# An attention stage's hand-placed pieces moved within the round, one output bank and three projection banks

## The reference, cut to what matters

```python
x = L0_attn_x                                   # 16 batches, 512 rows, 256 features
xn = _layernorm(x)
x = x + _L0_attn_ref(xn, ...)  + _L0_ffn_ref(xn, ...)
# _L0_ffn_ref:
x = x + mla(rmsnorm(x, w_ln1), ...)             # 16 heads of 16, causal softmax attention from low-rank
                                                # latents, with rotary halves, then W_o
x = x + moe(rmsnorm(x, w_ln2), ...)             # a shared expert on each row, and 2 of 7 routed experts
# _L0_attn_ref: a selective state-space scan (convolution, softplus, 512 steps of a clipped state)
```

## Time and profile before

| what | value |
| --- | --- |
| three executions | 4342.56, 4370.46, 4334.35 us |
| the profiled execution | 4341.7 us, its span 4339.9 us |
| mean granted clock of TensorE | 0.939 |
| PE, DVE, ACT, POOL busy, whole span | 86%, 68%, 58%, 51% |
| attention, 0 to 1710 us: PE busy | 1397.9 us |
| attention, 0 to 1710 us: DVE, ACT, POOL busy | 794.8, 650.9, 542.0 us |
| end of rounds 0 and 13 | 200.5 and 1499.1 us |

### The profile page before, as it was taken

One profiled execution on the slowest core, in us unless ns is written; L12 is line 12 of the kernel. 1 busy time (PEld: TensorE's weight loads), 2 busy tenths in 40 slices (PEclk: granted clock), 3 DMA queues, 4 the chain that ended last, 5 costly groups with the idle time before them and its releaser, 6 DMA issues. The chain is left out here.

```text
span 4339.9 us, 70850 instructions
## 1 busy us (share of the span) xinstructions
PE 3742.1 (86%) x22264; PEld 2767.9 (64%) x22264; DVE 2956.6 (68%) x5456; ACT 2513.7 (58%) x6505; POOL 2196.6 (51%) x1115
## 2 busy tenths in 40 slices
PE   5888888888888874899969999998999998999986
PEld 2344444444444442777758888887888887888876
DVE  3454454555444522222259999999999999999998
ACT  1443343434343441233358888888888888888874
POOL 3223333333333322000038788778778778878774
PEclk8899998999898987999989999999999999999998
DMA  3322222222232312666622212212222222222221
GB/s 91 98 80 84 80 92 86 88 80 81 79 101 81 93 46 75 199 208 208 211 92 98 88 68 100 93 66 97 93 70 93 93 81 82 93 88 75 93 83 38
DMA packets 286365, 417.03 MB, mean 96 GB/s; under 512 B 78261, under 2 KB 250678, under 8 KB 263672
## 3 DMA queue, kind: packets, MB, share of 16 engines
q1 hardware_dynamic: 273048, 381.12, 27.2%
q0 software_dynamic: 12288, 33.57, 2.2%
q10 hardware_dynamic: 864, 0.10, 0.0%
HBM read 330.63 MB, written 83.17 MB: 95 GB/s over the span
## 5 line engine op out<-in xcount | busy, mean ns | idle before, releaser
L1536 POOL TENSOR_TENSOR m_ub<-m_Bb,m_dtx 128x2048 f32<-128x2048 f32 x254 | 1156.9, 4566 | 280.3 <-PE m_Y L1904 176.4
L1645 ACT ACTIVATE m_dA<-m_dt,m_a_neg 128x128 f32<-128x128 f32 x4096 | 1211.1, 388 | 129.4 <-DVE m_S L1756 129.0
L1904 PE MATMUL m_Y<-m_ub,m_ident 128*128 128x128 f32 x8192 | 955.8, 278 | 62.4 <-DVE m_ub L1733 62.0
L1904 PEld LDWEIGHTS m_Y<-m_ub,m_ident 128*128 128x128 f32 x8192 | 939.3, 194 | 73.1 <-DVE m_ub L1733 72.8
L543 ACT ACTIVATE f_pt<-f_X 128x512 f32<-128x512 f32 (+1 forms) x704 | 371.8, 555 | 730.3 <-PE f_X L845 699.1
L618 DVE TENSOR_REDUCE f_nm<-f_Y 128x1 f32<-128x512 f32 (+3 forms) x896 | 434.0, 531 | 378.3 <-PE f_Y L845 354.1
L1748 DVE SCALAR_TENSOR_TENSOR m_PR<-m_dA,m_S 128x512 f32<-128x512 f32 x512 | 355.9, 695 | 25.7 <-POOL m_ub L1536 7.4
L1748 DVE SCALAR_TENSOR_TENSOR m_S<-m_dA,m_PR 128x512 f32<-128x512 f32 x512 | 354.8, 693 | 12.0
L1756 DVE CUSTOM_DVE_ANT_1 m_S<-m_S,m_ub 128x512 f32<-128x512 f32 x512 | 353.3, 690 | 0.6 <-issue 0.6
L1756 DVE CUSTOM_DVE_ANT_1 m_PR<-m_PR,m_ub 128x512 f32<-128x512 f32 x512 | 353.3, 690 | 0.2 <-DVE m_PR L1748 0.2
L828 PE MATMUL f_Y<-f_kst,f_qst 96*128 96x512 bf16 (+3 forms) x1024 | 256.2, 331 | 109.0 <-DVE f_nm L618 90.4
(11 more groups left out here) (234 smaller groups left out, 6369.2 us busy)
## 6 DMA issues: line engine op xcount, KB each, us to landing
m_Bb<-m_bc_dram SPq DMA_DIRECT2D x64, 1024.0 KB, 4.6
m_Cb<-m_bc_dram SPq DMA_DIRECT2D x64, 1024.0 KB, 6.4
f_parts_dram<-f_parts SPq DMA_DIRECT2D x32, 768.0 KB, 4.1
f_kst<-f_parts_dram SPq DMA_DIRECT2D x192, 128.0 KB, 2.6
f_qst<-f_parts_dram SPq DMA_DIRECT2D x192, 128.0 KB, 2.6
e_rows<-sorted_rows SPq DMA_DIRECT2D x70, 256.0 KB, 2.8
e_wg<-Wg SPq DMA_DIRECT2D x70, 256.0 KB, 2.9
e_wu<-Wu SPq DMA_DIRECT2D x70, 256.0 KB, 4.0
```

The lines of the kernel that those rows point to most:

```text
L1536: pool.tensor_tensor(ub[:, h, i, :, :], Bb[:, s, :, :], dtx[:, m, None, s * SN:(s + 1) * SN].to_broadcast([P, NST, SN]), ALU.mult).then_in ...
L1645: last = act.activation(dA[:, h, i, n, :], dtt[:, par, m, s * SN:(s + 1) * SN], ACT.Exp, scale=a_neg[:, m, n:n + 1])
L1904: last = pe.matmul(Y[:, i * SN:(i + 1) * SN], ident[:, :], ub[:, h, 1 + i, n, :], start=False, stop=(n == NST - 1), skip_group_check=True)
```

## The change

- **Pieces cut and moved.** T, ht and route become two pieces each, kq four for each head group, wo four. Nearly all places change: `d` goes from places 51 and 55 to 3 and 5 of the next round (stage -2), T from 15 to 8 and 9, lat from 18 to 12, kq of group 0 from 21 and 24 to 14, 16, 18, 18, kq of group 1 from 45 and 47 to 20, 22, 33, 33, wo from 25 to 25, 27, 29, 31, ht from 33 to 38 and 39, g and u from 37, 39, 42, 43 to 46, 49, 52, 55, rank from 40 to 52, nmt from 53 to 56, pfx from 47 to 58, keep from 32 and 58 to 27 and 44. scat (12 and 19), ym1 (18) and nm (50) stay.
- **Statistics a round earlier.** `xload` and `bn` work on batch n+3, at places 18 and 59; POOL's scalars of that norm are a kind of their own, `bnc`, at place 0 of the next round. There is one more round, -3, and rounds 2 to 11 are the loop; 12 and later are written out.
- **Banks.** One O bank instead of two, three Z banks instead of two. `oc` of a group now comes after the third s2 item of the next group instead of the sixth, and the first pv of a group waits for the copy of the group before. With it the pieces so, sl, rp, ro, rl, ym of the first pair of groups start at 35 instead of 39.
- **Numbering.** `place` counts each bank's uses by itself, and each round starts at bank 0 of each ring.

```diff
-    BANKS = {ring: [pb(f"f_{ring}{i}", [P, SEQ]) for i in range(2)] for ring in ("X", "Y", "Z")}
-    O = [pb(f"f_O{i}", [P, SEQ]) for i in range(2)]
+    DEPTH = {"X": 2, "Y": 2, "Z": 2, "Z": 3}
+    BANKS = {ring: [pb(f"f_{ring}{i}", [P, SEQ]) for i in range(DEPTH[ring])] for ring in ("X", "Y", "Z")}
+    O = pb("f_O", [P, SEQ])
...
-                if kb == 1 and g > 0:
-                    S2_ITEMS.append(("oc", g - 1, 0))
+            if n == 2 and kb == 0 and g > 0:
+                S2_ITEMS.append(("oc", g - 1, 0))
...
-    STAGE["scat"] = -2
+    STAGE.update({"scat": -2, "d": -2, "xload": 3, "bn": 3})
...
-    for n, kind, i, j in ((0, "xload", 0, 0), (0, "mvx", 0, 0), (0, "sl1", 1, 0), (1, "stack1", 1, 0), (4, "mvs", 0, 0), (6, "rp1", 1, 0), (7, "ro1", 1, 0), (8, "bn", 0, 0),
-                          (11, "h1", 0, 0), (12, "scat", 0, 0), (12, "rl1", 1, 0), (13, "h1a", 0, 0), (15, "T", 0, 0),
-                          (18, "lat", 0, 0), (18, "ym1", 1, 0), (19, "scat", 1, 0), (21, "kq", 0, 0), (24, "kq", 0, 1), (25, "wo", 0, 0),
-                          (26, "split", 0, 0), (28, "mid", 0, 0), (29, "h2", 0, 0), (30, "h2a", 0, 0), (31, "xrload", 0, 0),
-                          (32, "keep", 0, 0), (33, "ht", 0, 0), (35, "route", 0, 0), (36, "lg", 0, 0), (36, "xn", 0, 0), (37, "g", 0, 0), (37, "stack", 0, 0),
-                          (39, "u", 0, 0), (40, "rank", 0, 0), (42, "g", 1, 0), (43, "u", 1, 0), (45, "kq", 1, 0),
-                          (47, "kq", 1, 1), (47, "pfx", 0, 0), (49, "split", 1, 0), (50, "nm", 0, 0), (51, "d", 0, 0), (53, "mid", 1, 0), (53, "nmt", 0, 0),
-                          (55, "d", 1, 0), (58, "keep", 1, 0)):
+    for n, kind, i, j in ((0, "mvx", 0, 0), (0, "bnc", 0, 0), (0, "sl1", 1, 0), (1, "stack1", 1, 0), (3, "d", 0, 0), (3, "h1", 0, 0), (4, "mvs", 0, 0), (5, "d", 1, 0), (5, "h1a", 0, 0),
+                          (6, "rp1", 1, 0), (7, "ro1", 1, 0), (8, "T", 0, 0), (9, "T", 1, 0), (12, "scat", 0, 0), (12, "rl1", 1, 0), (12, "lat", 0, 0),
+                          (14, "kq", 0, 0), (16, "kq", 0, 1), (18, "kq", 0, 2), (18, "kq", 0, 3), (18, "ym1", 1, 0), (18, "xload", 0, 0), (19, "scat", 1, 0),
+                          (20, "kq", 1, 0), (20, "split", 0, 0), (22, "kq", 1, 1), (23, "mid", 0, 0), (25, "wo", 0, 0), (27, "wo", 1, 0), (27, "keep", 0, 0),
+                          (29, "wo", 2, 0), (31, "wo", 3, 0), (33, "kq", 1, 2), (33, "kq", 1, 3), (33, "xrload", 0, 0), (34, "h2", 0, 0), (35, "h2a", 0, 0),
+                          (35, "split", 1, 0), (37, "stack", 0, 0), (38, "ht", 0, 0), (39, "ht", 1, 0), (39, "mid", 1, 0), (42, "route", 0, 0), (43, "route", 1, 0), (44, "lg", 0, 0),
+                          (44, "keep", 1, 0), (45, "xn", 0, 0), (46, "g", 0, 0), (49, "u", 0, 0), (50, "nm", 0, 0), (52, "rank", 0, 0), (52, "g", 1, 0), (55, "u", 1, 0),
+                          (56, "nmt", 0, 0), (58, "pfx", 0, 0), (59, "bn", 0, 0)):
...
-    FIRST, LAST = -2, BATCH + 1
+    FIRST, LAST = -3, BATCH + 1
...
-        with nc.Fori(1, BATCH // 2 - 1, engines=[eng.engine], hint_back_edge=True) as g:
+        with nc.Fori(1, BATCH // 2 - 2, engines=[eng.engine], hint_back_edge=True) as g:
...
-                if g >= 2 or not isinstance(b, int) or b > 0:
-                    pe.wait_ge(o_copied, NG * b + g - 1)
+                if g > 0 or not isinstance(b, int) or b > 0:
+                    pe.wait_ge(o_copied, NG * b + g)
...
-                last = pe.matmul(O[g % 2][j * VA:(j + 1) * VA, kb * P:SEQ], va[:, kb, g * HG + j, :], src[:, j * n:(j + 1) * n],
+                last = pe.matmul(O[j * VA:(j + 1) * VA, kb * P:SEQ], va[:, kb, g * HG + j, :], src[:, j * n:(j + 1) * n],
...
             if kind == "d":
                 for i in range(NS):
-                    pe.wait_ge(*used(("u", i), r))
+                    pe.wait_ge(*used(("u", i), before_(r)))
```

More of the change, by code:

```diff
@@ L141, in build_attn @@
                 S2_ITEMS.append(("pv", q - 1, 0))
-                if kb == 1 and g > 0:
-                    S2_ITEMS.append(("oc", g - 1, 0))
-    STAGE = {kind: 2 for kind in ("xload", "bn", "h1", "h1a", "T", "lat", "kq", "split", "mid", "keep", "stack")}
+            if n == 2 and kb == 0 and g > 0:
+                S2_ITEMS.append(("oc", g - 1, 0))
+    STAGE = {kind: 2 for kind in ("bnc", "h1", "h1a", "T", "lat", "kq", "split", "mid", "keep", "stack")}
     STAGE.update({kind: 1 for kind in ("stack1", "s1", "nm", "nmt", "v")})
@@ L192, in build_attn @@
     NUMBERS = {(n, ring): numbered(n, ring) for n in range(FIRST, LAST + 1) for ring in BANKS}
-    FULL = 1
+    FULL = 2
     def index(r):
@@ L201, in place, with uses @@
         ring = ring_of(k)
+        depth = DEPTH[ring]
+        def uses(m, bank):
+            return (len(NUMBERS[m, ring]) + depth - 1 - bank) // depth
         n = index(r)
         if isinstance(n, int):
[L204 to L208, removed]
+            at = NUMBERS[n, ring][k]
+            bank = at % depth
+            return bank, sum(uses(m, bank) for m in range(FIRST, n)) + at // depth
+        at = NUMBERS[FULL, ring][k]
+        bank = at % depth
+        first = sum(uses(m, bank) for m in range(FIRST, FULL)) + (r[1] - FULL) * uses(FULL, bank) + at // depth
+        return bank, r[0] * (2 * uses(FULL, bank)) + first
     def before_(r):
@@ L570, in do @@
                     act.wait_ge(w_loaded, W_ALL)
-                for k in range(KM):
-                    read(("T", k), h1T[:, k, :], lambda bank: bank[:, :], ACT.Copy, scale=ln1[:, k:k + 1])
+                read(("T", i), h1T[:, i, :], lambda bank: bank[:, :], ACT.Copy, scale=ln1[:, i:i + 1])
             if kind == "lat":
@@ L595, in do @@
                 act.wait_ge(pv_done, NG * TT * b + TT * (i + 1))
-                act.activation(yT_[:, parity(kind, r), i, :], O[i % 2][:, :], ACT.Copy).then_inc(o_copied, 1)
+                act.activation(yT_[:, parity(kind, r), i, :], O[:, :], ACT.Copy).then_inc(o_copied, 1)
             if kind == "ht":
-                for k in range(KM):
-                    read(("ht", k), h2T[:, k, :], lambda bank: bank[:, :], ACT.Copy, scale=ln2[:, k:k + 1])
+                read(("ht", i), h2T[:, i, :], lambda bank: bank[:, :], ACT.Copy, scale=ln2[:, i:i + 1])
             if kind == "lg":
@@ L772, in full, with transposed @@
             ins.then_inc(full_sem(k, r), 1)
-        def transposed(kind, r, src):
-            for k in range(KM):
-                bank = free((kind, k), r)
-                for t in range(TT):
-                    last = pe.transpose(bank[:, t * P:(t + 1) * P], src[:, t, k * P:(k + 1) * P], ident[:, :])
-                full((kind, k), r, last)
+        def transposed(kind, k, r, src):
+            bank = free((kind, k), r)
+            for t in range(TT):
+                last = pe.transpose(bank[:, t * P:(t + 1) * P], src[:, t, k * P:(k + 1) * P], ident[:, :])
+            full((kind, k), r, last)
         def project(kind, i, j, b, r):
@@ L798, in project @@
                     pe.wait_ge(q_scaled, 1 + 16 * 2 * PARTS)
-                g, first, second = i, ("kq", i, j, 0), ("kq", i, j, 1)
+                g, part = i, j % 2
                 if j == 0:
@@ L802, in project @@
                     pe.sem_inc(taken)
-                bank = free(first, r)
+                bank = free(("kq", g, j // 2, part), r)
                 if j == 0:
@@ L807, in project @@
                         last = pe.matmul(bank[:, :], w_kra[:, k, g, :], h1T[:, k, :], start=False, stop=(k == KM - 1))
-                    full(first, r, last)
-                    bank = free(second, r)
+                elif j == 1:
                     for k in range(KM):
                         last = pe.matmul(bank[:, :], w_krb[:, k, g, :], h1T[:, k, :], start=(k == 0), stop=(k == KM - 1))
-                    full(second, r, last)
                 else:
-                    full(first, r, pe.matmul(bank[:, :], w_q[LAT:P, 0, g, :], lat[LAT:P, :], start=True, stop=True))
-                    bank = free(second, r)
-                    full(second, r, pe.matmul(bank[:, :], w_q[LAT:P, 1, g, :], lat[LAT:P, :], start=True, stop=True))
+                    last = pe.matmul(bank[:, :], w_q[LAT:P, part, g, :], lat[LAT:P, :], start=True, stop=True)
+                full(("kq", g, j // 2, part), r, last)
             if kind == "v":
```

96 lines of the change are left out of this document (52 added, 44 removed).

## The result

The changed kernel takes 4228.09 us in the median of four executions (4219.77 to 4241.81), where the kernel before beside it took 4356.51 (4334.35 to 4370.68): a ratio of 0.971, with a 95% interval from 0.965 to 0.977. Run once more in a later session it gave 4222.47 us and 0.972 (0.966 to 0.977). The forecast was 4252, with 4220 to 4285 as the range of that case and 4175 to 4345 as the range over the rivals.

The account below looks back on a forecast made before the run. PE's in-order queue and what stops it were taken to bound attention. Terms sum to -6.3 us a round, x 13 = -82, with the ends -90: 4342.56 to 4252 us; own range 4220 to 4285, over the rivals 4175 to 4345.

Parts of the forecast that it names:

- Y waits, -4.1: PE's waits for DVE to read a Y bank, 5.9 us a round, become 1.8: -4.1 us a round.
- The maxima, -2.1: PE's waits for the split of the maxima, 2.1 us a round, are hidden by nmt six places behind nm: -2.1.
- the transposes, -1.3: PE's waits before transposes, 1.7 us a round, become 0.4: -1.3 us a round.
- at most one instruction of 2.35 us, which lies beside PE work: At POOL's ym of pair 0 meeting DVE's rank: a delay of at most 2.35 us, covered by PE work.
- X waits, +4.2: PE's waits for ACT to read an X bank, 2.3 us a round, grow to 6.5 as ACT stands for POOL: +4.2.
- One output bank, 0: A single O bank costs nothing, since ACT copies it before the fourth exponential, which the waiting pv needs anyway: 0.
- rival (d): O copies lie bare on PE: four a round, some 1 us each, +4 us a round, 4304 us; chance 0.05.
- Clock, -3.0: PE's mean granted clock rises from 0.93 to 0.96 in rounds 1 to 13: -3.0 us a round.
- Ends, -8: Fill and drain: rounds 0 and 14 save 5 us, one loop turn fewer some 3: -8 us in all.
- Rival (a): Clean spread: ACT's stands don't reach PE, X waits stay 2.3, clock 0.97; 4190 to 4215 us; chance 0.25.
- Rival (b): No measurable change: Y stalls become X stalls one for one, -1 to -2 us a round, about 4325 us; chance 0.17.
- Rival (c): Slower: PE gets 1.2 GHz between two new stalls at mid 0 and split 1, +6 us a round, about 4400; chance 0.10.

Follow-up runs that it names:

- keep_late: The changed kernel with the 768 KB store keep 1 back at place 58 instead of 44; ratio 0.965 to the kernel before.
- rank_early: The changed kernel with rank at place 48 instead of 52; ratio 0.960 to the kernel before.
- pair_late: The changed kernel with the six softmax-sum pieces of pair 0 four places later, the O copy staying early; ratio 0.963 to the kernel before.
- bare_copy: The changed kernel with the O copy directly ahead of the pv that needs it, and pair 0's softmax-sum pieces four places later; ratio 0.965 to the kernel before.
- after_again: Second trace of the changed kernel, with nothing altered; the repeat run gave 4222.47 us, ratio 0.972 to the kernel before.
- scat_late: The changed kernel with scat 1 (four indirect DMAs on POOL) at place 24, behind mid 0, instead of 19; ratio 0.960 to the kernel before.

## Why the prediction was right, and where not

**Y waits, -4.1.** Measured -4.6 (5.9 to 1.2 a round), and by places too: the first 20 us of a round give 2.4 for the 2.3 forecast (1.4 and 0.9), the stretch behind the projection 2.0 for the 1.8. The rest went at 68 to 84 us, less new waits at 52 to 60. Of the three transfers blamed at the round's start, keep_late acquits the 768 KB store alone. DVE's wait for the sums, which was to go, is 3.8 us in all after 18.2.

**The maxima, -2.1, and the transposes, -1.3.** Measured -1.9 and -1.6; the cast shrank from 2065 to 188 ns once POOL's subtraction was elsewhere.
The Trainium skill, GPSIMD Engine Reference, Specifications, has GpSimd contend for the SBUF interfaces with those VectorE instructions that are in a two-port mode or have two SBUF inputs; the trace agrees, with 0.36 against 2.45 us for one DVE form without and beside a POOL product, and so do the counts at the end of this document.

**The step that failed: "at most one instruction of 2.35 us, which lies beside PE work".** The size was right to a tenth (2.36), the cover was not there: behind rank on DVE stands the read of g 1, and PE needs that bank at pfx. 1.6 us a round of idle and, by rank_early and pair_late, some 6 us a round at 1.2 GHz, which is 3 us more. The sum had 0. "No wait in the earlier trace rows is for the reader of a Z bank" was read from the kernel before, where rank stood twelve places earlier.

**X waits, +4.2.** Measured +2.8 (2.4 to 5.2). "mid" 0 by the chain given: ACT stood 5.6 us for the 4 expected, PE 2.0 for the 2.6. "split" 1 cost 2.2 for the 3.3, for another reason than given: ACT's own h2a ahead of it, which the step did not count.

**One output bank, 0.** Right on these places: there is no wait on the copy in the changed kernel, and rival (d) is out. The rule set against it in the prediction holds once the copy is late: 3.0 us a round in bare_copy.

**Clock, -3.0: mis-sized.** PE's busy time fell by 2.4, but that it comes near the forecast is luck. The time at 1.2 GHz fell from 15.0 to 12.3 us, which is worth 1.3, and the clock rose to 0.933 and not to 0.96; the two repairs of the pfx wait show some 3 us more that a round could have had. The other 1.1 of the busy time is not the clock: 0.3 are the two "d" pieces that left the 13 rounds, and 0.8 no run explains.

**Ends, -8: mis-sized.** Measured -31, of which -21.8 lie before the end of round 0. Round -1 alone, 62.3 us before and 49.0 after, in the windows view of the kernel before and then of the changed one:

```profile
62.80:125.10 62.30, 48.12 (x156) 20.05 (x156) 35.70 (x80) 9.23 (x13) 17.18 (x18) 0.69 0.27 81
```
```profile
59.70:108.70 49.00, 41.80 (x156) 18.76 (x156) 35.23 (x80) 9.46 (x13) 15.98 (x15) 0.78 0.39 121
```

The same 156 matmuls take 6.3 us less at a clock of 0.78 for 0.69, and idle time is 7.0 less: the waits on f_nm go from 7.7 to 4.5, and those for h and nmT (1.7 and 1.2) are gone. The prediction gave savings to rounds 0 and 14 and none to this one. Round 0 saved 5.4, the time to the first score fill 3.1. The start is the same in after_again (178.0 us to the end of round 0), but its tail is 239.6 us long instead of 232.5, so of the tail's 9.3 only some 2 are sure. The one loop turn fewer, which the prediction put here, shows inside the 13 rounds: PE's waits that the view puts down to "issue", most of them where the loop turns, go from 23.0 to 11.1 us.

Together: idle -5.0 where the terms had -3.3, busy -2.4 for -3.0, so -7.4 a round for -6.3. The named waits give -3.7 of the 5.0 (-4.6, -1.9, -1.6, +2.8, +1.6), those put down to "issue" another 0.9. With the ends it is 37 us less than the sum, and the experts and scan, where nothing was changed, take 5 us more in both traces of the changed kernel; the cause is open. Rival (a) expected ACT's stands to be hidden; scat_late shows they were not. Rival (b) had the gain eaten one for one; the X waits ate 2.8 of 8.1, and pfx 1.6. Rival (c) was wrong in size but not in kind: a small stall did slow the clock, at pfx.

## What to carry to other kernels

For each instruction that is moved, ask which instructions of the other engine it now runs beside, not only which queue it stands in, and look for PE's next need behind the one that stretches: parting one POOL product from DVE's rank was worth 1% of the kernel. A stall of 2 us that recurs in each round costs more than its length when a slow spell follows: about twice at pfx, 1.3 times at "mid" 0 (scat_late: 3.2 us of idle time and 0.9 lost at half speed). Repairs of an order written by hand are to be timed together too, since two good moves made a transfer and a small one meet.

## What the runs showed of the hardware

A small DVE instruction, of 0.2 to 0.4 us alone, takes 1.9 to 2.5 us when it begins just behind the start of a POOL product or subtraction of 128x1024 f32: it ends as POOL's does. Which forms are held this way can be counted in the 14 traces, over all DVE instructions of the first 1700 us that begin while a POOL TENSOR_TENSOR of over 1 us has more to run than they need alone. Held are all 206 whose operands are all in SBUF and that add, multiply or compare two of them, compare with a constant, cast or copy (f_cmp, f_chosen, f_picked, f_nm_part and their like). Held are none of 2708 others: reductions, reciprocals, the statistics, and sums and products with one operand in PSUM. Two that go on at their usual speed under the residual sum of 784.44 to 786.79 us in the changed kernel:

```profile
784.88 1.34 DVE L626 TENSOR_REDUCE f_nm<-f_Y 128x1 f32<-128x512 f32 x3
...
786.14 0.17 DVE L701 RECIPROCAL f_sc<-f_sc 128x4 f32<-128x4 f32 x1
```

So rank and the first cast of the maxima are at risk beside POOL, and the row maxima, DVE's largest share, are not.

Waits of PE of about 2 us before pfx were followed by 3.4 to 13.7 us at 1.2 GHz in seven of ten cases in one trace of the changed kernel and in five of ten in the other; over all variants a round had between 5.5 and 17.1 us at 1.2 GHz with the same work. Both numbers move with single pieces that are off PE's queue.
